# Eight groups of six slices and one matmul for the last rows: another layout of the one-hot row pick in five graph convolutions

## The reference

```python
# second layer, twice
x_src = x[src]
msg = sum over r of where(edge_type == r, x_src @ W[r], 0)
out = segment_sum(msg * norm, dst) + x @ root + bias
# fourth layer, three times
W = (edge_attr @ ew + eb).reshape(E, 16, 16)
msg = einsum('ei,eio->eo', x[src], W)
out = segment_sum(msg, dst) + x @ rw + rb
```

## Time and profile before

| | us |
|---|---|
| median of 3 runs (12178.45 to 12192.49) | 12188.94 |
| profiled execution, its own time | 12082.95 |
| its span | 12081.0 |
| stage r0, first to last pick | 1068 |
| stage r1 | 1046 |
| stages c0, c1, c2 | 1051, 1052, 1049 |
| the rest of the span | 6815 |

### The profile page before, as it was taken

One profiled execution on the slowest core, in us unless ns is written; L12 is line 12 of the kernel. 1 busy time (PEld: TensorE's weight loads), 2 busy tenths in 40 slices (PEclk: granted clock), 3 DMA queues, 4 the chain that ended last, 5 costly groups with the idle time before them and its releaser, 6 DMA issues. The chain is left out here.

```text
span 12081.0 us, 167867 instructions
## 1 busy us (share of the span) xinstructions
PE 9816.9 (81%) x42305; PEld 6821.8 (56%) x42305; DVE 9313.9 (77%) x14722; ACT 8267.0 (68%) x16314; POOL 7589.7 (63%) x6233
## 2 busy tenths in 40 slices
PE   5888888888885079878997688888899689969996
PEld 2333333333332057766775578777777577757775
DVE  7999999999997877764554699997666567656665
ACT  4777777777775057755775488885677467746774
POOL 4555555555556368876776677773677567756775
PEclk7666666666666589988998799998999799979997
DMA  3444444444444267765775111111888578858884
GB/s 117 178 178 177 176 177 178 178 178 178 178 176 138 91 244 269 260 229 188 249 248 167 50 46 44 45 45 26 276 287 290 182 260 293 284 183 268 287 289 161
DMA packets 750362, 2256.05 MB, mean 187 GB/s; under 512 B 272537, under 2 KB 420654, under 8 KB 673806
## 3 DMA queue, kind: packets, MB, share of 16 engines
q10 hardware_dynamic: 161280, 1027.68, 24.1%
q1 hardware_dynamic: 388638, 984.49, 21.7%
q0 software_dynamic: 200304, 242.20, 9.0%
HBM read 1321.84 MB, written 931.93 MB: 187 GB/s over the span
## 5 line engine op out<-in xcount | busy, mean ns | idle before, releaser
L592 POOL DMA_INDIRECT h<-in_x,idx x1568 | 2022.0, 1290 | 1731.9 <-DMA efT<-in_edge_attr_t 1269.9
L676 ACT ACTIVATE PX<-PX,h 128x16 f32<-128x16 f32 x12544 | 2510.5, 293 | 10.2 <-issue 3.8
L625 PE MATMUL PS<-M,minus_ident 128*128 128x512 f32 x1568 | 1417.5, 1030 | 313.9 <-DVE M L710 313.4
L1997 PE MATMUL PS<-mhr,lhs 128*128 128x392 f32 x6272 | 1262.6, 357 | 197.2 <-DVE lhs L2161 171.4
L1479 PE MATMUL PS<-every_weight,dstf 112*128 112x144 f32 (+1 forms) x8960 | 1273.8, 285 | 161.5 <-DVE dstf L1611 114.3
L1479 PEld LDWEIGHTS PS<-every_weight,dstf 112*128 112x128 f32 x8960 | 1223.3, 192 | 317.3 <-DVE dstf L1611 145.3
L1964 POOL DMA_INDIRECT myg<-node_table,mix x784 | 1103.7, 1408 | 447.7 <-issue 230.7
L2060 ACT ACTIVATE mhr<-mhb 128x1568 fp32r<-128x1568 bf16 x784 | 1142.1, 1505 | 294.6 <-DVE mhb L2151 239.0
L1997 PEld LDWEIGHTS PS<-mhr,lhs 128*128 128x128 f32 x6272 | 1152.5, 194 | 282.1 <-ACT mhr L2060 143.8
L613 PE MATMUL PS<-waug,efT 17*128 17x256 f32 x6272 | 1042.3, 535 | 300.0 <-DVE e L688 257.5
L613 PEld LDWEIGHTS PS<-waug,efT 17*128 17x128 f32 x6272 | 612.8, 252 | 1034.4 <-issue 495.6
(11 more groups left out here) (419 smaller groups left out, 20434.1 us busy)
## 6 DMA issues: line engine op xcount, KB each, us to landing
softmax_maxima<-M SPq DMA_DIRECT2D x196, 1024.0 KB
softmax_denominators<-ST SPq DMA_DIRECT2D x196, 1024.0 KB
softmax_numerators<-ST SPq DMA_DIRECT2D x196, 1024.0 KB
one_hot_rows_of_sources<-r0hb ACTq DMA_DIRECT2D x224, 896.0 KB
r1hb<-one_hot_rows_of_sources ACTq DMA_DIRECT2D x224, 896.0 KB
c0hb<-one_hot_rows_of_sources ACTq DMA_DIRECT2D x224, 896.0 KB
c1hb<-one_hot_rows_of_sources ACTq DMA_DIRECT2D x224, 896.0 KB
c2hb<-one_hot_rows_of_sources ACTq DMA_DIRECT2D x224, 896.0 KB
```

The source lines that it names most:

```text
L592: PO.indirect_dma_start(h[b.k][:, at(q), :], None, io["x"], bass.IndirectOffsetOnAxis(ap=idx[b.k][:, q:q + 1], axis=0))\
L625: mm = PE.matmul(PS[0:CH, 4 + n, :], minus[:, :], M[b.k % 2][:, n::4, :], start=False, stop=True)
L676: act = S.activation(PX[b.k][:, 1, t, D * i:D * i + D], PX[b.k][:, 0, t, D * i:D * i + D], ACT.Copy, scale=h[b.k][:, t, i:i + 1])
L1997: mm = PE.matmul(PS[:, 6 + k, 0:A7 // 2], lhs[(G * b.k + q) % 2][:, 2 * two + r, part, :], hr[(2 * G * b.k + j) % 4][:, r, k * A7 // 2:(k ...
```

## The change

The nodes are laid out anew: node number = 768 x group + 128 x slice + partition, with 8 groups (A8) of 6 slices (KB). This covers 6144 nodes. The 128 numbers from 6144 on, the last table rows, get a seventh slice of the one-hot of their own and one matmul more: `last_parts` has 80 columns, the big part in columns 0 to 15, zeros, and the small part in columns 64 to 79. An edge to one of these nodes takes group 0 on partitions 0 to 63 and group 4 on partitions 64 to 127, so that the mask keeps both parts and the weigh adds them. A group of edges now has 12 pick matmuls with 128 columns of weights and one with 80: 13 for 14. The mask and the weigh use all 128 partitions in place of 112.

There are thus two group-number tables (`pick_a[0]`, `pick_a[1]`), each broadcast to 64 partitions, and in `setup_vector` three tiles in place of two: three more instructions on 128x1568, one more comparison in the series, 13 transposes and 13 copies more, and two DMAs more. Since 39 transposes don't fit in PSUM's 32 places, the last 7 wait for copies.

```diff
@@ -28,7 +28,8 @@
-A9, KT = 7, 7
+A8, KB, KT = 8, 6, 7
+ROWS = 128 * KB
...
@@ -371,21 +373,31 @@
...
+            V.tensor_copy(pab[2][:, :], si[:, :]).then_inc(*vd.up())
+            V.wait_ge(*vd.now())
+            V.tensor_scalar(pab[0][:, :], pab[2][:, :], float(ROWS), None, ALU.is_ge).then_inc(*vd.up())
+            V.tensor_scalar(pab[1][:, :], pab[2][:, :], float(A8 * ROWS), None, ALU.is_ge).then_inc(*vd.up())
+            for k in range(2, A8):
...
             V.wait_ge(*pT_up.now())
-            V.wait_ge(*t2v.next(2 * NT))
+            turned_of = t2v.taken
             for k in range(NT):
-                for n in TWO:
+                for n in range(3):
+                    if 3 * k + n in (0, 32):
+                        V.wait_ge(t2v.sem, turned_of + min(3 * k + n + 32, 3 * NT))
                     V.tensor_copy(pT[0:wd[k], k, n, 0:CH], spread_at(k, n)).then_inc(*pT_up.up())
...
@@ -1317,6 +1338,9 @@
+        PICKS = 2 * KB + 1
+        LOWEST = 6
...
-                SP.dma_start(ra[half][:, :], rows(b, half, pick_a)).then_inc(h_ra[half].sem, 16)
+                groups_of = pick_a[:, some(b, NG + 16 * half, 16), :].rearrange("h t c -> h (t c)")
+                SP.dma_start(ra[half][:, :], bc(groups_of, 64, 1)).then_inc(h_ra[half].sem, 16)
...
                     for m in range(m0, m1):
-                        mm = PE.matmul(PS[0:A9 * D, 4 + q % 2, :], parts[:, m % 2, m // 2, :],
-                                       hot_[q % 2][:, m // 2, :], start=(m == 0), stop=(m == 2 * KT - 1))
-                    if m0 < m1 == 2 * KT:
+                        if m == LOWEST:
+                            PE.matmul(PS[0:64 + D, 4 + q % 2, :], last_parts[:, :], hot_[q % 2][:, KB, :], start=False, stop=False)
+                            continue
+                        n = m - (m > LOWEST)
+                        mm = PE.matmul(PS[:, 4 + q % 2, :], parts[:, n % 2, n // 2, :],
+                                       hot_[q % 2][:, n // 2, :], start=(m == 0), stop=(m == PICKS - 1))
+                    if m0 < m1 == PICKS:
...
-                    at = 2 * KT if both else 9
+                    at = PICKS if both else 9
...
-                    V.scalar_tensor_tensor(out=mx[q % (1 + LAG)][:, :], in0=ra[q // 4][0:A9 * D, 512 * (q % 4):512 * (q % 4) + 512],
-                                           scalar=pick_row[0:A9 * D, 0:1], in1=PS[0:A9 * D, 4 + q % 2, :],
+                    V.scalar_tensor_tensor(out=mx[q % (1 + LAG)][:, :], in0=ra[q // 4][:, 512 * (q % 4):512 * (q % 4) + 512],
+                                           scalar=pick_row[:, 0:1], in1=PS[:, 4 + q % 2, :],
```

More of the change, by code:

```diff
@@ L219, in program @@
         si = sb("srci", [CH, T], I32, setup)
-        pab = [sb(f"pab{k}", [CH, T], F32, setup) for k in TWO]
+        pab = [sb(f"pab{k}", [CH, T], F32, setup) for k in range(3)]
         NT = (T + 127) // 128
-        pT = sb("pT", [128, NT, 2, 128], I16, setup)
+        pT = sb("pT", [128, NT, 3, 128], I16, setup)
         wd = [min(128, T - 128 * k) for k in range(NT)]
@@ L254, in setup_sync @@
             SP.dma_start(flags, fl[:, :, :]).then_inc(*s_init.up(16))
-            SP.wait_ge(pT_up.sem, 2 * NT + 1)
-            for n, d_ in enumerate((pick_a, pick_b)):
+            SP.wait_ge(pT_up.sem, 3 * NT + 1)
+            for n, d_ in enumerate((pick_a[0, :, :], pick_a[1, :, :], pick_b)):
                 SP.dma_start(d_[0:FULL, :].rearrange("(k q) c -> q k c", q=128), pT[:, 0:NT - 1, n, :])\
@@ L398, in setup_tensor @@
             for k in range(NT):
-                for n in TWO:
+                for n in range(3):
+                    if 3 * k + n == 32:
+                        PE.wait_ge(pT_up.sem, 1 + 32)
                     PE.transpose(spread_at(k, n), pab[n][:, 128 * k:128 * k + wd[k]], ident[0:CH, 0:CH])\
                         .then_inc(*t2v.up())
-            PE.wait_ge(*pT_up.next(2 * NT + 1))
+            PE.wait_ge(*pT_up.next(3 * NT + 1))
         setup_sync()
@@ L1366, in conv @@
             LAG = 2 if both else 1
-            mx = [dstf[0:A9 * D, 512 * k:512 * k + 512] for k in range(1 + LAG)]
+            mx = [dstf[:, 512 * k:512 * k + 512] for k in range(1 + LAG)]
             c_g = c_gs[both]
@@ L1479, in weigh_rows @@
                         mm = PE.matmul(weighed(q)[:, r, 0:R * D], mx[q % (1 + LAG)][:, 128 * r:128 * r + 128],
-                                       every[0:A9 * D, 0:R, :].rearrange("p r o -> p (r o)"))
+                                       every[:, 0:R, :].rearrange("p r o -> p (r o)"))
                     mm.then_inc(h_sel.sem, 1)
                 def steps(nx, b):
-                    at = 2 * KT if both else 9
+                    at = PICKS if both else 9
                     for q in range(HG):
```

39 lines of the change are left out of this document (25 added, 14 removed).

## The result

| | before | after |
|---|---|---|
| median, us (4 runs each) | 12183.69 | 13249.78 |
| lowest to highest | 12169.68 to 12192.49 | 13246.33 to 13259.13 |
| ratio, 95% interval | | 1.088 [1.087, 1.089] |
| stages r0, r1, c0, c1, c2 | 1068, 1046, 1051, 1052, 1049 | 1177, 1235, 1327, 1328, 1327 |

The changed kernel is 1066 us slower; the forecast was 165 us faster and the range ended at 12135. Between the two profiled executions the span grows by 1170 us, of which 1128 lie in the five stages. All the rest is 42 us, nearly all of it ahead of r0, whose first pick starts 39 us later (4349 against 4310).

A forecast was written before the change was run, and what follows sets the result against it. PE was taken to set the pace for about 943 of a c stage's 1051 us, the rest stalls. Gains of 135 (c stages), 32 (r1) and 12 (r0) less 14 setup made 165: 12189 to 12024 us, range 11945 to 12135.

The forecast's parts named there:

- Part 3: Mask and weigh on 128 partitions and the two-table group-number loads: costed at nothing, DMA share rising from 0.88 to 0.93.
- Part 1: One pick matmul less per group on PE's path: 0.23 us, 51.5 us a stage, 258 us for five.
- The rival of the wider load: 128-column weight loads lie on PE's path: gain only 0 to 0.07 us per group, time 12125 to 12203; chance 0.07.
- Part 2: Main layout's 12 picks load 128 weight columns instead of 112: hidden under matmuls, cost nothing, at most 0.24 us a group.
- The stage terms: Gains in the five stages: 45 us in each of three c stages, 32 in r1, 12 in r0.
- Stage r0: Stage r0 goes at GpSimd's pace in about half its blocks: gain 12 us, bounds 0 and 30.
- GpSimd binds everywhere: GpSimd limits all stages: gain 17 us per c stage, 26 in r1, 0 in r0; time 12126; chance 0.18.
- Setup: Serial work ahead of the first layer, with extra comparisons, transposes, copies and DMA issues: 14 us slower, bounds 9 and 18.
- TensorE's clock drops: Idle PE time in r0 and r1 puts picks at 1.2 GHz in 150 of 448 groups: time 12293; chance 0.06.
- I am wrong if the stalls grow by what the picks lose.: Stated sign of failure: PE's stalls, about 108 us per c stage, lengthen by the time the removed picks save.

The follow-up runs named there:

- the repaired kernel: Changed kernel with each group-number load as two DMAs, one per table: 11311 us against 11643 for the unchanged kernel (0.971); elsewhere 12030 against 12077 (0.996).
- the 14-pick kernel: Changed kernel with two DMAs per group-number load and a fourteenth matmul over zero weights put back: 11438 us against 11630 unchanged, 0.984.
- the padded one: Unchanged kernel, 14 picks and old load, weights zero-filled from 112 to 128 columns, mask and weigh on 128 partitions: 11424 us against 11630, 0.982.
- e6: Unchanged kernel with each group-number load as two DMAs of 64 partitions from the same table: 12111 us against 12078, 1.003.

## Why the prediction was wrong, point by point

- **Part 3, the step that failed.** "I cost all three at nothing", and "if the two-row source made the loads slower, DMA has room: share 0.88". I did see that the source had two rows, and reasoned with the mean share over 16 engines. A mean doesn't say how a single transfer is spread. The same bytes on 2 engines need 64 x 0.18 = 11.5 us of a half block on each of them, on top of 14.4 us of other work, and that is over the 18.8 us that a half block took. The share stood in the earlier trace rows and the pattern in the diff; the diff's outermost dimension and the time of a packet were the missing pieces. Price: 1197 us.
- **Part 1, the pick's time.** Right: 4.21 to 4.02 us per group, and 4.25 to 4.02 from 14 wide picks to 13. The rival of the wider load is refuted by the spacing, and **Part 2** holds: 14 wide picks in place of 14 narrow ones cost 0.04 us a group (4.21 to 4.25), 3 ns a pick. The Trainium skill's columns / 1.2 ("TensorE: Matmul & The Clock Gate", section "LDWEIGHTS (loading the stationary operand)") would have made an estimated 13 ns a load of it, if loads were on the path. The trace shows the load itself longer by 14 (median 174 to 188 ns) and mostly hidden; by the same rule of the Trainium skill the loads themselves would take an estimated 93 and 107 ns, which the trace does not bear out.

```profile
L1498 PEld LDWEIGHTS PS<-c0hot,parts x2688: 186/188/338, 8831.0 to 10157.7; 128*128 128x128 f32 x192
```

- **The stage terms**, by the repaired kernel without late signals (14 to 13 picks): c stages 30 each where I had 45, r1 40 where I had 32, r0 15 where I had 12. Sum 145 us in the stages of the two traces, 136 by the medians, for 179. In the c stages the DMA engines or the gathered rows absorb what I gave to full gain, and I never made the sum for the DMA engines: my own estimate of a 0.93 share was a warning that PE was within 7% of another limit.
- **Stage r0**, "the gathers are drawn out by VectorE's work, of which the change removes none; at most 30 us". The bound was wrong: r0 loses 85 us by the width alone, as its gathers go from 1260 to 1111 ns. That GpSimd set the pace was read rightly; that its duration was a constant was not.
- **GpSimd binds everywhere** (0.18) was right in part: in the comparisons without late signals VectorE waits for gathered rows in c0, 111.7 us before and 66.5 with 13 picks. It was wrong in what follows, since the wide layout itself shortens the gathers and moves that limit: r1 lost 65 us and the c stages 60 from before to 13 picks, where the rival had 26 and 17.
- **Setup**, 14 us: right. The last copy ends 12.4 us later (13 forecast), and the 14-pick kernel lies 14 us above the padded one:

```profile
40.19 10.92 DVE L382 SCALAR_TENSOR_TENSOR pab<-pab 128x1568 f32<-128x1568 f32 x6
...
70.75 1.47 DVE L399 CAST pT<-PS 128x128 int16<-128x128 f32 x7 [1.85 <-PE PS L414]
```

- **TensorE's clock drops** (0.06) was the only rival on the slower side. The granted clock did fall, to 0.86 in the c stages. It follows the stalls, and PE is busy only 12 us more in c0 than before: it isn't where the 276 us went. So "slower" came true, by a mechanism that no rival of mine held.
- **"I am wrong if the stalls grow by what the picks lose."** Something of the kind shows even with the load repaired, with late signals: 13 wide picks 12030 us, 14 wide picks 11995. In c0 the period accounts for 224 x 4.02 = 900 of 1038 us in the one and 224 x 4.25 = 952 of 1043 in the other, so that the stalls are 91 us with 14 picks and 138 with 13. I took seven of 52 us for that. But the two kernels differ by more than the pick: the 13 picks have the two-DMA load, which cost the kernel of before 33 us in all (e6), and the longer setup of 14 us. How much of the lost gain is theirs and how much the stalls', no run tells. VectorE waits for remote 145.6 and 145.4 us in the two:

```profile
DVE dstf L1641 <- remote: 145.6, 43, 8.4
```
```profile
DVE dstf L1614 <- remote: 145.4, 40, 9.8
```

  These waits are as long with less work on PE. What the releaser is, why it is late in some comparisons and not in others, and what one pick is worth there (the 14-pick kernel with the repaired load was never run with late signals) stays open.

## What to carry to other kernels

When a change rewrites a load's access pattern, read its outermost dimension before its bytes: it decides how many of the 16 DMA engines carry it, and the slowest of those, with everything else queued on it, sets the landing. A mean DMA share can't show this, neither as room before nor as load after; runs of low share while an engine waits for a landing do. And before crediting an engine's saved work in full, add up the next limit's work per block, DMA engines included, and treat the duration of an instruction beside other traffic as something that the change may move.

## What the runs showed of the hardware

- A load of 512 KB in 4 KB packets lands after 5.5 us on 16 DMA engines, 15 on 8, 24 on 4 and 36 on 2, in c0, in the midst of this kernel's traffic. Two engines alone moved 50 to 52 GB/s.
- The same 4 KB packets take on average in c0 160 to 167 ns where one DMA has the 128 partitions outermost and 181 with two tables of 64, but 276 ns as two DMAs of 64 partitions, 259 with 16 tables, 250 with 8 and 204 with 4.
- Gathers on GpSimd get 12% shorter in r0 (1260 to 1111 ns) and 5% in c0 (1165 to 1101 ns) when weights, mask and weigh beside them are 128 wide in place of 112.
- One kernel has two levels of time, 4% apart (11631 to 11643 and 12077 to 12184 us), the same within a comparison. Every trace of the longer has waits for a releaser called remote and holds about half of the semaphore records, and none of the shorter does either. A change's ratio differs between them: 0.971 and 0.996 for the same two kernels.
